# Second convolution: accumulators by column parity, linear term and squares by F(2,3) along the columns

## The reference

```python
x = x + L0(gn(x))      # gn: each channel of each image to mean 0, variance 1
x = x + L1(gn(x))

# L0: a 3x3 conv, shifted nine times and weighted per channel, plus a 5x5 conv and biases.
#     Away from the border it is one 5x5 convolution.
# L1: a quadratic 3x3 layer. For each pixel the ten numbers (1, the 9 pixels of its 3x3
#     neighbourhood) are multiplied with each other, and the 100 products go with
#     filters (32, 32, 10, 10) into 32 output channels:
spot = concatenate([ones, patches(x, 3)])            # 10
feat = spot[..., :, None] * spot[..., None, :]       # 10 x 10
out = einsum('bcyxf,ocf->boyx', feat, filters.reshape(O, C, 100))
```

## Time and profile before

| | us |
|---|---|
| median of 3 runs | 315.72 |
| lowest, highest | 315.37, 581.59 |
| the profiled execution, its own time | 314.26 |
| its span, first to last instruction | 312.5 |
| TensorE (PE) busy in it | 291.7 (93%) |
| VectorE (DVE) busy | 213.2 (68%) |
| ScalarE (ACT) busy | 88.4 (28%) |
| GpSimd (POOL) busy | 32.0 (10%) |

### The profile page before, as it was taken

One profiled execution on the slowest core, in us unless ns is written; L12 is line 12 of the kernel. 1 busy time (PEld: TensorE's weight loads), 2 busy tenths in 40 slices (PEclk: granted clock), 3 DMA queues, 4 the chain that ended last, 5 costly groups with the idle time before them and its releaser, 6 DMA issues.

```text
span 312.5 us, 14558 instructions
## 1 busy us (share of the span) xinstructions
PE 291.7 (93%) x6976; PEld 147.5 (47%) x6976; DVE 213.2 (68%) x198; ACT 88.4 (28%) x145; POOL 32.0 (10%) x76
## 2 busy tenths in 40 slices
PE   0699999899999999999999999999999999999990
PEld 0233443443356664365464556447444745554640
DVE  2899899969999998549888553590023896981121
ACT  4432027986258302300000407840000000000181
POOL 7915950000000000000000000000000000000000
PEclk9999999999999999999999999999999999999996
DMA  6972000000000000000000002540000000000047
GB/s 205 386 177 56 4 3 2 5 2 4 2 4 2 4 4 3 2 4 2 4 4 2 4 2 62 112 103 4 4 2 2 4 2 4 2 4 2 4 103 168
DMA packets 7626, 11.51 MB, mean 37 GB/s; under 512 B 5392, under 2 KB 5520, under 8 KB 7440
## 3 DMA queue, kind: packets, MB, share of 16 engines
q1 hardware_dynamic: 5104, 9.59, 11.6%
q10 hardware_dynamic: 2464, 1.01, 1.4%
HBM read 6.40 MB, written 4.19 MB: 34 GB/s over the span
## 4 chain that ended last, share of the span: by engine, by line
PE 84%; DVE 6%; ACT 3%; DMA 2%; issue 1%; SPq 1%; DVEq 0%
PE acc L851 68%; PE acc L878 14%; ACT raw L476 3%; DMA raw<-in_x 2%; DVE stats L685 2%; PE acc L929 2%; DVE plane L703 1%; DVE product L637 1%; ACT product L466 1%; DVE scaled L605 0%; SPq L296 0%; DVE norm L700 0%; SPq L303 0%; DVE mean_var L690 0%; DVE product L730 0%
## 5 line engine op out<-in xcount | busy, mean ns | idle before, releaser
L851 PE MATMUL acc<-product,weight 32*32 32x512 f32 (+1 forms) x4416 | 182.8, 598 | 0.0
L775 DVE TENSOR_TENSOR product<-plane 128x4096 f32<-128x4096 f32 x24 | 105.2, 4424 | 48.8 <-PE acc L851 48.8
L851 PEld LDWEIGHTS acc<-product,weight 32*32 32x32 f32 (+1 forms) x4416 | 98.4, 111 | 79.7 <-issue 56.4
L507 ACT ACTIVATE raw<-acc,offset_by_strip 32x512 f32<-32x512 f32 x36 | 24.4, 679 | 99.6 <-PE acc L851 99.1
L878 PE MATMUL acc<-product,middle 32*64 32x512 f32 (+1 forms) x576 | 28.9, 595 | 0.0
L851 PE MATMUL acc<-plane,weight 32*32 32x512 f32 (+1 forms) x512 | 26.1, 599 | 0.6 <-DVE product L637 0.6
L723 DVE TENSOR_SCALAR raw<-acc,offset_by_strip 32x512 f32<-32x512 f32 x12 | 9.1, 757 | 24.1 <-PE acc L851 23.8
L476 ACT ACTIVATE raw<-product 32x512 f32<-32x512 f32 x36 | 24.5, 681 | 2.8 <-DVE product L637 2.3
L534 ACT ACTIVATE product<-plane 128x4096 f32<-128x4096 f32 x2 | 7.3, 3632 | 50.8 <-PE acc L851 48.0
L685 DVE BATCH_NORM_STATS2 stats<-raw 128x6 f32<-128x512 f32 x32 | 19.7, 680 | 2.5 <-DMA raw<-in_x 2.3
L605 DVE TENSOR_TENSOR product<-plane 128x2048 f32<-128x2048 f32 (+1 forms) x8 | 18.6, 2339 | 0.0
(11 more groups left out here) (93 smaller groups left out, 145.8 us busy)
## 6 DMA issues: line engine op xcount, KB each, us to landing
raw<-in_x SPq DMA_DIRECT2D x8, 512.0 KB, 8.2
out<-raw SPq DMA_DIRECT2D x12, 256.0 KB, 3.0
filters_in<-in_L_conv_filters SPq DMA_DIRECT2D x4, 400.0 KB, 7.0
out<-product SPq DMA_DIRECT2D x8, 64.0 KB, 2.5
out<-product ACTq DMA_DIRECT2D x8, 64.0 KB, 2.7
w_in<-in_L_conv_w ACTq DMA_DIRECT2D x4, 100.0 KB, 3.9
w_in<-in_L_conv_w ACTq DMA_DIRECT2D x2, 36.0 KB, 1.9
w_in<-in_L_conv_w SPq DMA_DIRECT2D x2, 36.0 KB, 2.3
```

What stands on the lines that cost most here:

```text
L507: last = nc.scalar.activation(strip_rows(g, r, s, h), strip_acc(s, h, r), ACT.Identity, bias=offset_by_strip[32 * s:32 * s + 32, r, g:g + 1])
L775: nc.vector.tensor_tensor(product_rows(n), inner(g, 0, H), shifted(g, PRODUCTS[k]), ALU.mult)\
L851: return nc.tensor.matmul(acc[32 * s:32 * (s + strips), h, r, :], weights[32 * r:32 * r + 32, t:t + strips, :] .rearrange("p t c -> p (t c ...
```

## The change

Only L1 and what serves it changes. The two halves of PSUM are now the even and the odd output columns, as in L0, and a tile holds two "streams", one for each half (`half_stream`, `both_halves`): 33 words per row, 32 columns and a zero. A matmul still has 512 pixels, 16 rows of 32.

- F(2,3) along columns, for the linear term and the squares in both groups, for product (0,1) in group 1: with even column a, odd column b of each pair and its neighbours, and taps w0, w1, w2, TensorE applies (w0+w1+w2)/2 to a+b and (w0-w1+w2)/2 to b-a, which serve both outputs, then w0 to (left neighbour - b) for the even one and w2 to (right neighbour - a) for the odd one. That is four columns of taps where there were six; for (0,1), with two taps, three (`next_sum`, left, right) where there were four. In group 0 the linear a+b is not made: its taps go over both parities of the plane, so its linear term takes five.
- The shared parts are copied out of PSUM by ScalarE (`keep_sum`, `keep_cross`), and `mix` on VectorE makes their sum and difference with the offset added. `evict` is VectorE's alone: the accumulator plus the shared part, every second word of `result`, which is `raw[0]` for both groups.
- VectorE makes the streams (`linear_sum` to `next_right`, 7 in group 0, 10 in group 1), and the combined taps (`mixed_taps`). Products are in a new order; product tiles and `raw` are now all homes of streams (`UNIT_HOME`).
- Of `take`, 24 copies go to ScalarE's `spread`. The filters, their sums and L0's second group's halves share one tile, `arena`.
- Stores: 16 of 128 KB for each group, once both parities of an image are there; those of group 1 on two queues.

The diff, cut to its core:

```diff
+UNIT_HOME = ({LINEAR: 1, SQUARE: 3, SQUARE_MIXED: 0, NEXT: 2, LINEAR_SIDES: "raw0", SQUARE_SIDES: 1,
+              7: 3, 8: 0, 9: "raw0", 10: 1, 11: 2, 12: 3, 13: 0, 14: "raw0", 15: 1, 16: 2, 17: 3},
+             {LINEAR: 0, SQUARE: "raw1", SQUARE_MIXED: 1, NEXT: 2, LINEAR_SIDES: 3, SQUARE_SIDES: 0, NEXT_SIDES: 1,
+              7: "raw1", 8: 2, 9: 3, 10: 0, 11: 1, 12: "raw1", 13: 2, 14: 3, 15: 0, 16: 1, 17: "raw1"})
...
+PRODUCTS = ((0, 0), (0, 1), (1, 1), (1, -1), (0, 2), (2, 2), (2, -2), (2, 1), (1, 2), (2, -1), (1, -2), (2, 0), (1, 0))
...
+        def both_halves(g, u):
+            return view(home(g, u), HALF_AT, (HPITCH, H), (HALF_LEN, 2), (1, HALF_W))
+
+        def plane_halves(g, shift=0):
+
+            return view(plane[g], PLANE_AT + shift, (PITCH, H), (1, 2), (2, HALF_W))
...
+        def store(eng, g, r, strips):
+
+            for s in strips:
+                y = SIDE_ROWS * (s // 2) + 1 - s % 2
+                eng.dma_start(out[GROUP * g + r][:, y:y + SIDE_ROWS - 1:2, :],
+                              result[32 * s:32 * s + 32, 2 * CHUNK * r:2 * CHUNK * (r + 1)]
+                              .rearrange("p (y x) -> p y x", x=W)).then_inc(stored, 16)
...
+            def keep_sum(g):
+
+                act.wait_ge(weight1_ready, 1)
+                act.wait_ge(edge_ready, 1)
+                act.wait_ge(shared_done, g + 1)
...
+                nc.scalar.activation(kept_sum, part_acc(0), ACT.Copy).then_inc(shared_kept, 1)
+
+            def keep_cross(g):
+
+                wait_used(act, g, SQUARE_MIXED)
...
             square(0)
+            spread(1, 0, (0,))
             copy_edges(1, ROW_SIDES)
-            spread(1, 0, range(EVEN_ON_ACT))
+            spread(1, 0, (1,))
             copy_edges(1, COLUMN_SIDES)
+            keep_sum(0)
+            spread(1, 0, (2,))
+            keep_cross(0)
+            spread(1, 0, (3,))
+            spread(1, 1, range(GROUP))
             std(3)
             normalise(3)
             spread_offset()
             square(1)
...
+            keep_sum(1)
+            keep_cross(1)
+            for r in range(GROUP):
+                act.wait_ge(evicted, 3 * GROUP + r + 1)
+                store(act, 1, r, (2, 3))
...
+            def mix(g):
+
+                dve.wait_ge(shared_kept, 2 * (g + 1))
+                dve.wait_ge(offset_spread, 1)
...
                 for r in range(GROUP):
...
+                    last = nc.vector.scalar_tensor_tensor(image(even_shared, r), image(kept_sum, r),
+                                                          offset_by_strip[:, r, g:g + 1], image(kept_cross, r),
+                                                          ALU.add, ALU.add)
+                step(last)
+                for r in range(GROUP):
+                    last = nc.vector.scalar_tensor_tensor(image(kept_sum, r), image(kept_sum, r),
+                                                          offset_by_strip[:, r, g:g + 1], image(kept_cross, r),
+                                                          ALU.add, ALU.subtract)
+                last.then_inc(mixed, 1)
+
+            def evict(g, odd):
+                dve.wait_ge(mixed, g + 1)
+                dve.wait_ge(half_done, 2 * g + odd + 1)
+                if g == 1:
+                    dve.wait_ge(stored, 16 * GROUP * STRIPS)
+                shared = kept_sum if odd else even_shared
+                for r in range(GROUP):
+                    nc.vector.tensor_tensor(view(result, 2 * CHUNK * r + odd, (W, CHUNK // HALF_W), (2, HALF_W)),
+                                            acc[:, odd, r, :].rearrange("p (y x) -> p y x", x=HALF_W),
+                                            shared[:, CHUNK * r:CHUNK * (r + 1)].rearrange("p (y x) -> p y x", x=HALF_W),
+                                            ALU.add).then_inc(evicted, 1)
...
             halve(1, "right")
+            mixed_taps()
             whole_and_cross(1)
...
             finish_odd(1)
-            multiply(0, 1)
-            take(1, 0, range(EVEN_ON_ACT, GROUP))
-            take(1, 1, range(GROUP))
-            for k in range(2, PRODUCT_BUFS):
-                multiply(0, k)
+            dve.wait_ge(plane_act, NG + 1)
+            square_sum(0)
+            linear_cross(0)
+            square_cross(0)
+            linear_left(0)
+            multiply(0, NEXT)
+            square_left(0)
+            linear_right(0)
+            square_right(0)
+            multiply(0, 7)
+            multiply(0, 8)
             finish_x1(1)
             step(statistics(1, lambda n: None, every))
             normalise(3)
             make_offset()
...
+            multiply(0, 9)
+            multiply(0, 10)
+            mix(0)
+            for u in range(11, LAST_UNIT + 1):
+                multiply(0, u)
+            dve.wait_ge(plane_act, NG + 2)
+            dve.wait_ge(borders, 6)
+            linear_sum(1)
+            linear_cross(1)
+            square_sum(1)
+            square_cross(1)
+            evict(0, 0)
+            multiply(1, NEXT)
+            evict(0, 1)
+            linear_left(1)
+            linear_right(1)
+            square_left(1)
+            square_right(1)
+            next_left(1)
+            next_right(1)
+            for u in range(7, 10):
+                multiply(1, u)
+            mix(1)
+            for u in range(10, LAST_UNIT + 1):
+                multiply(1, u)
+            evict(1, 0)
+            evict(1, 1)
...
                 if g == 0:
                     pe.wait_ge(even_ready, NG)
-                    linear(g, 0, False, True)
+                    for half in (0, 1):
+                        column(0, plane_pixels(0, half), every_row, sum_taps[0][:, 0:3, :], half == 0, False, PAIRS)
                     edges0(1, ROW_SIDES)
-                    linear(g, 0, True, False)
...
+                    for half in (0, 1):
+                        column(0, plane_pixels(0, half), every_row, sum_taps[0][:, 0:3, :], False, False, SINGLES)
                     edges0(1, COLUMN_SIDES)
...
+                    pe.wait_ge(borders, 5)
+                    mixed_unit(g, 0, "square", SP, stop=True).then_inc(shared_done, 1)
                     pe.wait_ge(edges_copied, 2 * NG)
...
+                mixed_unit(g, 1, "linear", SP if g else PS, start=True).then_inc(unit_used, 1)
+                mixed_unit(g, 1, "square", PS if g else SP, stop=True).then_inc(unit_used, 1)
+
+                pe.wait_ge(shared_kept, 2 * g + 1)
+                side_unit(g, 0, "linear", SP if g else PS, start=True)
+                side_unit(g, 0, "square", PS if g else SP)
```

More of the change, by code:

```diff
@@ L276, in wait_product_free @@
[L276 to L280, removed]
-            else:
[L282 to L292, removed]
+        result = raw[0]
@@ L737, in take, with take_odd @@
+            def take_odd(g, images):
+                odd, half = 1, odd_half(g)
+                dve.wait_ge(odd_ready, g + 1)
                 for r in images:
@@ L989, in _, with mixed_unit, side_unit, taps1 @@
             rest0(1, PAIRS_FIRST)
-            def linear(g, h, pairs, start):
-                for n, ix in enumerate((-1, 1, 0)):
-                    three = middle1[g] if ix == 0 else weight1[:, 3 * (ix + 1):3 * (ix + 2), :]
-                    column(h, plane[g], PLANE_AT, ix, range(-1, 2), three, start and n == 0, False, pairs)
-            def taps1(g, h, k, pairs, stop=False):
+            every_row = range(-1, 2)
+            SINGLES, PAIRS = False, True
+            def mixed_unit(g, j, name, forms, start=False, stop=False):
+                sum_or_cross = "cross" if j else "sum"
+                pe.wait_ge(stream_made, made(g, f"{name} {sum_or_cross}"))
+                if name == "linear":
+                    taps = (cross_taps if j else sum_taps)[g][:, 0:3, :]
+                else:
+                    taps = (cross_taps if j else sum_taps)[0][:, 3:6, :]
+                for pairs in forms:
+                    last = column(j, stream_pixels(g, UNIT_OF[name][0], j), every_row, taps,
+                                  start and pairs == forms[0], stop and pairs == forms[-1], pairs)
+                return last
+            def side_unit(g, j, name, forms, start=False):
+                pe.wait_ge(stream_made, made(g, name + (" right" if j else " left")))
+                if name == "next":
+                    a = FIRST1[1] + 3 * j
+                else:
+                    a = {"linear": 0, "square": 9}[name] + 6 * j
+                for pairs in forms:
+                    last = column(j, stream_pixels(g, UNIT_OF[name][1], j), every_row, weight1[:, a:a + 3, :],
+                                  start and pairs == forms[0], False, pairs)
+                return last
+            def taps1(g, j, u, pairs, stop=False):
+                k = 1 if u == NEXT else u - 5
                 ys = rows_of(PRODUCTS[k])
@@ new lines, in _ @@
+                    pe.wait_ge(evicted, GROUP)
+                    mixed_unit(g, 0, "linear", PS, start=True)
```

(15 more changed lines are left out.)

428 lines of the change are left out of this document (234 added, 194 removed).

## The result

The changed kernel takes 305.29 us (median of 4; 304.6 to 305.6) where the kernel before took 315.94 beside it: a ratio of 0.967, 95% interval 0.964 to 0.969. One execution of the kernel before, of 581.59 us, is in its median of four, but not in the ratio; without it the median is 315.72. So the change gives 10.4 to 10.7 us, where 15.7 were forecast (315.72 to 300.0). The profiled execution took 305.6 us with a span of 303.9.

A forecast was written before the change was run, and what follows sets the result against it. TensorE was taken to bound L1: 22.7 us saved, less small waits and 5.4 us given back at the end, made the span 296.7 us for 312.5. That gave a median of 300.0 us, range 295 to 307.

The forecast's parts named there:

- The filter's saving: L1's matmuls: three columns of taps fewer in group 0 (8.5 us), five in group 1 (14.2 us), together 22.7 us.
- Form changes are no more frequent.: TensorE in L1: switches from pair to single matmuls were taken as no more frequent than before, so nothing was added.
- Matmuls on streams of 32 words a row are those of L0, so I price them alike.: L1's matmuls on 32-word rows priced like 64-word ones, from L878's 592 against 596 ns.
- The wait terms of group 0: TensorE in L1's group 0: about 0.7 us waiting for products, 0.8 us for the borders' copies, before 0.3.
- VectorE's schedule: VectorE in L1: a half stream 2.3 us, a product 4.36 us, mix 5.0 us with 3.4 and 6.1 as ends.
- The tie: Group 0 of L1: products 11 to 16 ready about when TensorE wants them; about 0.7 us of wait in all.
- the warning about the clock: TensorE: should waits grow to several us, the clock may fall, and 1.2 GHz would lose more than the waits.
- Rival 1: VectorE late in group 0, then group 1: 303 us if two-half forms are 5% dearer, 309 at 10%; chance 0.15.
- Rival 2: TensorE saves less: short rows, step-two reads or PSUM copies cost something; half the saving lost gives 311 us; chance 0.07.
- The end: After the last matmul: 2.10 MB to store instead of 1.05, at 199 GB/s; 13.3 us instead of 7.9.
- The start of L1: TensorE starts L1 at 88.57 us as before; `mixed_taps` and keep_whole's new wait were taken to add 0.

## Why the prediction was right, and where it was off

- **The filter's saving.** Right in kind, and held up by the run with (0,1) applied directly: fewer columns, less time, TensorE still the bound. 5 and 3 columns at 2.84 us were 22.7 us; TensorE's L1 became 16.1 us shorter.
- **"Form changes are no more frequent."** This step failed. I compared the products, which looked alike, and didn't count the half streams. 19 more changes at 0.12 to 0.16 us are 2.3 to 3.0 us.
- **"Matmuls on streams of 32 words a row are those of L0, so I price them alike."** The term was mis-sized. The new rows have pitch 33, and all but one of L0's streams 32; the pitch alone is 1.2 + 1.5 us. The reading behind it was weak, too: 592 and 596 ns are the mean durations of one matmul out of several under way, over several of L0's streams together, and not what one more costs. The windows of L0's columns, 3.51 and 3.43 us, showed the difference.
- **The wait terms of group 0** (0.7 us for products, 0.5 for the borders): the list has 2.1 us for products and 0.6 for the borders. Those on products cost nothing; TensorE itself stood still for 0.38 us in all. Taken together: changes 1.0 to 1.3, pitch 1.2, less 0.7 for waits that were free, is 1.5 to 1.8 of the 1.8 missing in group 0; 1.3 to 1.8 and 1.5 are 2.8 to 3.3 of the 3.3 missing in group 1.
- **VectorE's schedule.** The prices of products and half streams hold to 0.1 us, and mix took 5.5 us instead of 5.0, between its bounds: an instruction of it takes 0.69 us in a row (2.74 to 2.79 for four), not 0.63.
- **The tie.** "Every microsecond late lengthens the kernel by one" is confirmed at unit 12 by the delay of 4.85 us, and so is the warning about the clock, which added 1.3 us. Unit 11 had 2.3 us of slack, where the prediction's times give 2.5 (153.2 less 150.7), and unit 12 at most 0.1, where they give 0.3 (155.4 less 155.1). Units 13 to 16 were not tried. Rival 1 did not occur.
- **Rival 2,** TensorE saves less than the columns say, is what happened in part: 16.1 of 22.7 us, for the two causes above; no wait for the copies out of PSUM is in the lists.
- **The end.** 12.6 us, forecast 13.3; 210 GB/s where I took 199. The direction and its cause are shown by the run with half of the stores.
- **The start of L1** was taken from one profile that lay 1.6 us below the median of three.

In the median the forecast was 300.0 and the measured time 305.3, inside the range of 295 to 307. In the profiled execution it was 298.5 and 305.6, so 7.1 us are missing there: 5.1 of L1 and 2.9 of its start, less 0.7 at the end. In the median the low start of the first profile was made good by the 1.46 us that the prediction added for the median, so L1's 5.1 us are nearly all of the 5.3. The direction and the way it comes about were forecast rightly. That the range held was in part luck: its upper end was drawn for rival 1, and what filled it were the changes of form and the rows.

## What to carry to other kernels

When a filter divides work into more and smaller units, count the changes between tile shapes on TensorE as instructions with a price of their own, and group equal shapes across units. When a new layout is priced by an old one, check the distance between the rows that TensorE reads and where they start, not only their length, and price it by windows of a whole column, not by the mean duration of one matmul. A wait of the weight loads that fits into the pause at a change of shape is free. To find the slack of a queue that feeds TensorE, compare when each unit starts, not how long TensorE waits: a lower clock hides waits, since the slowed work fills the time.

## What the runs showed of the hardware

- A change between 32x64 and 32x32 matmuls costs 0.12 us (22 more in the kernel before: 106.5 to 109.15 us) to 0.16 us (six fewer in the changed one: 95.61 to 94.66 us).
- fp32 matmuls of 16 rows of 32 words take 1.6% less in sum with row starts 256 bytes apart than with 264 (group 1: 93.19 against 94.66 us); where the first row starts changed with it. In L0 a column of pairs takes 3.43 us with pitch 32 and 3.51 with 33.
- With waits of 2.04 and 1.09 us, which ended 4.3 us apart, the granted clock averaged 0.66 over the 10 us from 160, then was 1.00 again. TensorE's busy time for the same records grew by 3.2 us.
- Stores in pieces of 256 bytes ran at 210 GB/s with the DMA engines full; 1.05 MB more cost 4.9 us.
